# One output bank, four projection banks, and the products with v at the end of TensorE's slot, in an attention kernel over 128 graphs

## The reference, cut to what matters

```python
h = max(layernorm(x), 0)                       # x: (128, 128, 384)
q, k, v = h @ Wq + bq, h @ Wk + bk, h @ Wv + bv   # 12 heads of 32 each
scores = q @ k^T / sqrt(32) + beta * adj       # per head, 128 x 128
scores = where(adj > 0, scores, -9e15)
out = x + softmax(scores) @ v                  # heads side by side
```

## Time and profile before

| | |
|---|---|
| median of three runs | 1078.22 us |
| the profiled execution | 1079.27 us |
| its span, first to last instruction | 1077.4 us |
| mean granted TensorE clock | 0.992 of full |
| TensorE busy | 1020.8 us (95%) |
| VectorE busy | 967.6 us (90%) |
| ScalarE busy | 884.5 us (82%) |
| GpSimd busy | 567.5 us (53%) |

### The profile page before, as it was taken

The page is one execution under the profiler, slowest core; times in us unless marked ns, Lnnn a source line. Parts: engine busy times, 40 slices in busy tenths (PEclk is TensorE's granted clock), DMA queues, the critical chain, the costliest instruction groups (busy, mean ns, idle before and its releaser), DMA issues. The chain is left out here.

```text
span 1077.4 us, 33776 instructions
## 1 busy us (share of the span) xinstructions
PE 1020.8 (95%) x10959; PEld 709.7 (66%) x10959; DVE 967.6 (90%) x4343; ACT 884.5 (82%) x2343; POOL 567.5 (53%) x756
## 2 busy tenths in 40 slices
PE   3899999999999999999999999999999999999986
PEld 2466676666666666666666667666666666667664
DVE  6579998999899999999999999999999999999897
ACT  3378888888888888888888888888888888888887
POOL 3645655445665445565444565544565544565431
PEclk9899999999999999999999999999999999999997
DMA  5454445554444554444554444554444554444441
GB/s 156 108 132 129 113 127 139 158 134 127 107 133 132 157 138 129 111 129 136 150 140 132 111 130 129 150 145 134 130 107 132 144 150 134 130 104 135 117 116 41
DMA packets 91038, 138.79 MB, mean 129 GB/s; under 512 B 15600, under 2 KB 66288, under 8 KB 90864
## 3 DMA queue, kind: packets, MB, share of 16 engines
q1 hardware_dynamic: 90336, 135.85, 47.1%
q10 hardware_dynamic: 528, 0.79, 0.2%
HBM read 35.91 MB, written 25.17 MB: 57 GB/s over the span
## 5 line engine op out<-in xcount | busy, mean ns | idle before, releaser
L523 ACT ACTIVATE probs<-biased,neg_max 128x128 f32<-128x128 f32 x1536 | 490.5, 390 | 146.9 <-DVE neg_max L638 115.5
L437 PE MATMUL ps_p<-hT,w 128*128 128x512 f16 x1728 | 423.5, 382 | 23.9 <-DVE hT L609 18.7
L638 DVE CUSTOM_DVE_ANT_0 biased<-ps_s,mask 128x128 f32<-128x128 f32 x1536 | 353.5, 286 | 75.8 <-PE ps_s L458 74.5
L336 POOL TENSOR_TENSOR on<-on,xb 128x384 f32<-128x384 f32 x128 | 128.0, 1000 | 380.9 <-DVE on L659 380.1
L437 PEld LDWEIGHTS ps_p<-hT,w 128*128 128x128 f16 x1728 | 167.5, 98 | 175.7 <-DVE hT L609 26.1
L644 DVE TENSOR_TENSOR pT<-ps_t,pT 128x512 f16<-128x512 f32 x384 | 263.3, 686 | 0.9 <-ACT pT L548 0.9
L466 PE MATMUL ps_t<-ident,probs 128*128 128x128 f32 x1536 | 245.4, 283 | 0.1
L548 ACT ACTIVATE pT<-ps_t 128x512 f16<-128x512 f32 x384 | 220.5, 574 | 1.0 <-PE ps_t L466 1.0
L437 PE MATMUL ps_p<-w,hT 128*128 128x384 f16 x1152 | 207.6, 326 | 0.0
L458 PEld LDWEIGHTS ps_s<-k_st,q_st 96*128 96x128 f16 x1536 | 117.5, 97 | 81.3 <-DVE neg_max L638 6.9
L481 PE MATMUL ps_o<-v,pT 128*128 128x33 f16 x1536 | 157.1, 179 | 8.9 <-DVE pT L644 5.2
(11 more groups left out here) (62 smaller groups left out, 1016.8 us busy)
## 6 DMA issues: line engine op xcount, KB each, us to landing
q_st<-qT SPq DMA_DIRECT2D x384, 96.0 KB, 2.2
k_st<-kT SPq DMA_DIRECT2D x384, 96.0 KB, 2.2
out<-on SPq DMA_DIRECT2D x128, 192.0 KB, 2.1
xs<-in_x SPq DMA_DIRECT2D x31, 768.0 KB, 5.0
adjs<-in_adj SPq DMA_DIRECT2D x32, 256.0 KB, 5.0
xs<-in_x ACTq DMA_DIRECT2D x1, 768.0 KB, 7.1
k_st<-in_L_gnn_Wq SPq DMA_DIRECT2D x1, 576.0 KB, 5.6
k_st<-in_L_gnn_Wk SPq DMA_DIRECT2D x1, 576.0 KB, 9.3
```

The costliest lines, as they stand in the source:

```text
L336: pool.tensor_tensor(on[:, j % 2, :], on[:, j % 2, :], xb[:, par, j, :], ALU.add).then_inc(added, 1)
L437: mm = pe.matmul(dst, stationary, moving, start=m == 0, stop=m == MMS - 1)
L523: act.activation(probs[:, odd, i, :], biased[:, odd, i, :], ACT.Exp, bias=neg_max[:, odd, i:i + 1], scale=-1.0).then_inc(exp_done, 1)
L638: dve.tensor_tensor_reduce(out=biased[:, odd, i, :], in0=ps_s[:, i * N:(i + 1) * N], in1=mask[:, gp, v // CH, :], scale=-1.0, scalar=3.0e3 ...
```

## The change

Three things change together. PSUM has eight banks: the two output banks become one (`ps_o`), and the projections get a fourth (`ps_p`, `PB = 4`, taken in turn over the whole program). TensorE does the products with v at the end of the slot and a slot sooner after the scores: chunk n-2 rather than n-3. VectorE does `invert_sums` right behind `bias_scores` and `scale_out` right behind `p_low`, ahead of `low_parts`. With one output bank, a graph's first products wait for the outputs of the graph just before it (`G * g + j` in place of `G * g + j - 1`).

```diff
-    PB = 3
-    BANK = [[(o + par) % PB for o in range(NB)] for par in range(2)]
+    PB = 4
+    def bank_of(s, o):
+        return (NB * s + o) % PB
...
-        ps_o = [ctx.enter_context(nc.psum_tensor(f"ps_o{b}", [P, 512], F32)) for b in range(2)]
-        ps_n = [ps_o[0], ps_o[1], ps_t[0]]
+        ps_o = ctx.enter_context(nc.psum_tensor("ps_o", [P, 512], F32))
+        ps_n = [ps_o, ps_p[3], ps_t[0]]
...
                 if s == 0 and o < PB:
-                    pe.wait_ge(h_low, o + 1)
+                    if o < CH:
+                        pe.wait_ge(h_low, o + 1)
+                    else:
+                        pe.wait_ge(qk_scaling, 4)
                     return
...
                 if c == 0:
-                    wait(pe, scaled, G * g + j - 1)
+                    wait(pe, scaled, G * g + j)
                     pe.wait_ge(v_split, G * g + j + 1)
                 pe.wait_ge(p_low_done, n + 1)
...
-                for u in range(SLOTS + (LAG + 3 if s == STEPS else 0)):
-                    scored, turning, valued = (chunk(s, par, u, behind) for behind in (0, 1, 3))
+                for u in range(SLOTS + (LAG + 2 if s == STEPS else 0)):
+                    scored, turning, valued = (chunk(s, par, u, behind) for behind in range(3))
                     if scored:
                         scores(*scored, (u - LAG) % 2)
-                    if valued:
-                        values_of(*valued, (u - LAG - 3) % 2)
                     if turning:
                         turn_probs(turning[0], (u - LAG - 1) % 2)
                     if proj:
                         piece(s, par, u, ahead)
+                    if valued:
+                        values_of(*valued, (u - LAG) % 2)
...
                     if scored:
                         bias_scores(*scored, (u - LAG) % 2)
+                    if ended:
+                        invert_sums(valued[1], valued[3] // CH)
                     if turned_late:
                         p_low(turned_late[0], (u - LAG) % 2)
+                    if ended:
+                        scale_out(valued[1], valued[3] // CH)
                     if u >= 1 and proj:
                         low_parts(s, par, u - 1, ahead)
...
-                    if ended:
-                        invert_sums(valued[1], valued[3] // CH)
                     if ahead and u < 2:
                         for j in range(2 * u, 2 * u + 2):
                             moments(s + 1, 1 - par, j)
-                    if ended:
-                        scale_out(valued[1], valued[3] // CH)
```

More of the change, by code:

```diff
@@ L393, in bank_free @@
                 if s == 0 and o < PB:
-                    pe.wait_ge(h_low, o + 1)
+                    if o < CH:
+                        pe.wait_ge(h_low, o + 1)
+                    else:
+                        pe.wait_ge(qk_scaling, 4)
                     return
-                before, last, here = s, o - 1, par
+                before, last = s, o
                 while True:
-                    if last < 0:
-                        before, last, here = before - 1, NB - 1, 1 - here
+                    before, last = divmod(NB * before + last - PB, NB)
                     unit = UNITS[last]
-                    runs = before < STEPS - 1 or unit[0] != "turn"
-                    if runs and BANK[here][last] == BANK[par][o]:
+                    if before < STEPS - 1 or unit[0] != "turn":
                         break
-                    last -= 1
                 kind, n = unit
@@ L422, in project @@
                 kind, n = UNITS[o]
-                bank = ps_p[BANK[par][o]]
+                bank = ps_p[bank_of(s, o)]
                 if first == 0:
@@ L447, in piece @@
                         bank_free(s, par, o)
-                        turn(s + 1, ps_p[BANK[par][o]], UNITS[o][1])
+                        turn(s + 1, ps_p[bank_of(s, o)], UNITS[o][1])
             def scores(n, g, gp, v, odd):
@@ L477, in values_of @@
                     h = c * HPC + i
-                    o = ps_o[j % 2][:, h * VW:(h + 1) * VW]
+                    o = ps_o[:, h * VW:(h + 1) * VW]
                     high, low = pT[:, odd, 0, i, :], pT[:, odd, 1, i, :]
@@ L563, in step @@
                             elif ahead:
-                                turn_high(s + 1, 1 - par, ps_p[BANK[par][o]], UNITS[o][1])
+                                turn_high(s + 1, 1 - par, ps_p[bank_of(s, o)], UNITS[o][1])
             for n in range(3):
@@ L627, in low_parts @@
                     elif UNITS[o][0] == "turn" and ahead:
-                        turn_low(s + 1, 1 - par, ps_p[BANK[par][o]], UNITS[o][1])
+                        turn_low(s + 1, 1 - par, ps_p[bank_of(s, o)], UNITS[o][1])
             def bias_scores(n, g, gp, v, odd):
@@ L645, in p_low, with outputs @@
                                   ALU.subtract).then_inc(p_low_done, 1)
-            def outputs(j):
-                return ps_o[j % 2][:, 0:HEADS * VW].rearrange("p (h d) -> p h d", d=VW)
+            def outputs():
+                return ps_o[:, 0:HEADS * VW].rearrange("p (h d) -> p h d", d=VW)
             def invert_sums(g, j):
@@ L653, in invert_sums @@
                 wait(dve, scaled, G * g + j - 1)
-                dve.reciprocal(inv_sum[:, j % 2, :], outputs(j)[:, :, HD]).then_inc(inverted, 1)
+                dve.reciprocal(inv_sum[:, j % 2, :], outputs()[:, :, HD]).then_inc(inverted, 1)
             def scale_out(g, j):
@@ L658, in scale_out @@
                 wait(dve, stored[j % 2], 16 * (G // 2 * g + j // 2))
-                dve.tensor_tensor(on[:, j % 2, :].rearrange("p (h d) -> p h d", d=HD), outputs(j)[:, :, 0:HD],
+                dve.tensor_tensor(on[:, j % 2, :].rearrange("p (h d) -> p h d", d=HD), outputs()[:, :, 0:HD],
                                   inv_sum[:, j % 2, :].rearrange("p (h o) -> p h o", o=1).broadcast_to([P, HEADS, HD]),
```

## The result

The changed kernel takes 1145.09 us (median of four runs, 1144.74 to 1145.5) against 1078.72 us for the kernel before in the same job. The ratio is 1.0615, with a 95% interval of 1.0597 to 1.0634: it is 6% slower. The forecast was slower, with 1169.5 us; the range was 1130 to 1192.

A forecast was written before the change was run, and what follows sets the result against it. TensorE was taken as the bound, with 30.9 of each 32.13 us step its own work. Added time of 72.2 + 1 + 3.4 + 12.7 + 2 = 91.3 us on 1078.22 gave 1169.5 us, range 1130 to 1192.

The forecast's parts named there:

- Own work of 30.9 us and 1.25 us of waits a step: TensorE in equal steps 2 to 30: a 32.13 us step is 30.9 us of its own work, 1.25 us waiting.
- k2's wait of 0.80 us: Slot 6: k2 waits for the bank VectorE reads as turn0; with the fourth projection bank the 0.80 us goes.
- The ring in common slots, 2.48 us, hidden: Scores, bias, low part, products, next scores once a slot: 2.48 us, hidden by a 2.52 us slot with 0.04 to spare.
- The ring where a graph ended, 3.23 us: Slots 2, 5, 8, 11: next graph's first products wait for VectorE's scaling with one output bank, ring 3.23 us.
- VectorE's backlog, slot 8: Slot 7 holds 3.36 us of VectorE work, so slot 8's bias starts at 1.42 and the slot lasts 4.07 us.
- The sum over 29 steps: Equal steps 2 to 30: 34.62 us against 32.13, 2.49 us more a step, 72.2 us over 29.
- The rest: Added time outside the equal steps: step 1 +1, step 31 +3.4, the last step +12.7, the start +2 us.
- the first rival: Clock falls in the last step: 0.54 us more a slot, 7.6 over 14, 1177 us; inside the forecast's range, 0.72.
- The pipe rule: VectorE's next operation waits until the pipe is empty: about 15 us more by estimate, left out of the sum.
- The backlog rival: VectorE starts every bias on time, so only four slots grow, each to 3.23 us: 1132 us, chance 0.10.

The follow-up runs named there:

- Number 12: The kernel of run 10 with the first k0 of step 0 held back until q0's low part: 1037.2 us, ratio 0.9611.
- run 8: The kernel before, its banks and TensorE order kept, with VectorE's outputs early and the late mask in slot 6: 1058.63 us, ratio 0.9812.
- run 9: The changed kernel with products of chunk n-3 right behind the scores and the late mask in slot 6: 1054.59 us, ratio 0.9769.
- runs 3 and 4: The changed kernel with VectorE's late mask moved from slot 7, to slot 10 (1131.0 us) and to slot 6 (1125.29 us).
- run 2: The changed kernel with the products of chunk n-3 right behind the scores: 1071.04 us, ratio 0.9923.
- run 6: The kernel before with only VectorE's reciprocal and scaling moved early, as in the change: 1069.71 us, ratio 0.991.
- run 10: The kernel of run 9 with TensorE's turned probabilities ahead of the products: 1038.51 us, ratio 0.9623.
- run 1: The changed kernel's order of both engines with the banks of before (two output, three projection): 1120.22 us, ratio 1.0378.

## Why the prediction was right in sign and mechanism, and where its sizes were off

- **Own work of 30.9 us and 1.25 us of waits a step.** Right, within 0.3. Number 12 has 30.67, with the 0.03 a slot that its order gains.
- **k2's wait of 0.80 us goes.** Right: slot 6 is 2.70. It was not worth its full price, though, since other waits take part of it back (numbers 8 and 9).
- **The ring in common slots, 2.48 us, hidden.** Right, by a hair: they last 2.48, and the ring itself 2.47, as the last step's first slot shows, where no projection hides it. They were forecast at 2.52, because I took TensorE's fixed 1.00 us unchanged; it is 0.97 in the new order. This term was 0.22 us a step too large.
- **The ring where a graph ended, 3.23 us.** This is the term that was mis-sized. Measured are 3.01 and 3.02. The reciprocal costs 0.15 and not 0.22, the low part 0.54 to the next start and not 0.60, and the release 0.05 and not the 0.12 that slot 9 of before suggested. Those three are 0.20 of the 0.21 us. Over four slots it is 0.81 us a step.
- **VectorE's backlog, slot 8.** Right in place and mechanism: its bias starts at 1.45 (forecast 1.42), and moving 0.66 us of mask away took 0.66 us from the slot. Forecast 4.07, measured 3.90: the ring is 0.20 shorter and the bias 0.03 later.
- **The sum over 29 steps.** Forecast 72.2 us, measured 45.4. The two terms above are 1.03 us a step or 30 us; a few steps with 0.15 to 0.35 us more in one slot give back 3.
- **The rest.** Forecast 1, 3.4, 12.7 and 2, measured 1.1, 2.4, 14.8 and 2.1. In the last step the shorter ring alone would have given 11.7 (four slots at 3.01, ten at 2.47, less 25.0); the clock brought it to 14.8: its mean in that stretch is 0.56, at the full 2.4 GHz until 1097.9 us and at 1.2 GHz behind that. That was the first rival, and it happened: common slots there last 2.72 us instead of 2.47 once the clock has fallen. I had priced it at 0.54 a slot, by doubling scores and products, and it costs 0.25. VectorE's bias starts 0.76 us behind the first score matmul instead of 0.56, and the twelve products there take 0.36 us, not twice 0.31, as TensorE's rows of the changed kernel there show by their starts:

```profile
1106.50 0.21 PE L483 MATMUL ps_o<-v,pT 128*128 128x33 f16 x1 [0.91 <-DVE pT L646]
...
1106.86 0.59 PE L460 MATMUL ps_s<-k_st,q_st 96*128 96x128 f16 x4
```

By the rule of the Trainium skill, "TensorE: Matmul & The Clock Gate", section "What's actually happening", activity is what releases the half clock. The trace agrees: the clock read 1.00 with TensorE at work in 30.08 of the 32.40 us of step 31, and fell after 4.7 us with 2.06 us of matmuls.

- **The pipe rule** would have added 15 us, and more with the low part inside the ring, which that estimate left out (0.09 us in each of four slots). The trace after again has the next instruction 0.54 to 0.60 us behind the start of a low part of 0.63 to 0.69, so leaving it out was right. The prediction gave only half of the rule. The Trainium skill, "VectorE: DVE Perf Modes", section "The DRAIN you can't avoid", adds that a next operation that is not held starts earlier. These rows agree with that sentence.

The backlog rival (1132 us) came closer to the measured time than the forecast did (13 us off against 24), yet by its number only: its mechanism, that VectorE starts every bias on time, is refuted by the 1.45 us in slot 8 and by runs 3 and 4. The forecast had some luck too: the slower clock of the last step gave 3 us that its sum did not hold.

## What to carry to other kernels

When a consumer is moved closer to its producer, write down the ring that this closes (scores, bias, low part, products, scores) with start-to-start times, and compare it with the shortest slot: here it fitted with some 0.01 us to spare (2.47 against 2.48), and one more link, the scaling, broke it. The same scarce bank cost less with a slot of slack between its reader and its next writer: 0.55 us a step in slots 3 and 9 (run 2 against run 6), 0.35 with the mask in slot 6 (run 9 against run 8), and next to nothing in run 10, where both slots last no longer than their own work. With the ring closed it cost 1.54 us a step, some 45 us, of which the fourth projection bank gave 0.81 a step back (run 1 against the changed kernel, 25 us apart in all). Smooth the helper engine's work over the slots first: moving one 0.66 us instruction gave 11 to 20 us in every version.

## What the runs showed of the hardware that was not expected

- An instruction on VectorE that reads what the one ahead of it wrote started later than an independent one. Reciprocal and scaling back to back start 0.26 us apart; with the independent low part behind the reciprocal it is 0.15 (537.18 to 537.33), and the low part's row is 0.63 instead of 0.69.
- With outputs late, TensorE waits 2.02 us in slot 8, and the clock read 0.50 (1.2 GHz) for a stretch in slot 9 behind it in 21 of 29 steps. In the changed kernel, which waits 1.18 us at that place, it read 1.00 in all of steps 2 to 30. The two kernels differ in the waits of slots 2, 5 and 11 as well.
- A free bank can cost time: with its first k0 moved ahead of the wait for GpSimd, TensorE idled 6.27 us in one piece instead of 4.31, ran the turn and the nine matmuls behind it at 1.2 GHz, and came to the first scores at 59.61 us instead of 57.51. Holding k0 back gave 1.3 us in number 10 (run 12).
